# A routed expert stage in which one bias product per tile becomes two products in all, and two engines share the taking out of gathered tiles

## The reference, cut to what matters

```python
# x: 1024 tokens of 128, already normalised once and passed in as input_features
aff = x @ centroids.T                      # 8 affinities
assign = argmax(aff, axis=1)
xs, es = x[order], assign[order]           # order = argsort(assign)
alpha = sigmoid(aff of the chosen expert)
for e in range(8):
    h = layernorm(xs, ln_g[e], ln_b[e])
    h = relu(h @ w1[e].T + b1[e])          # 128 -> 512
    ye = xs + h @ w2[e].T + b2[e]          # 512 -> 128
    y += where(es == e, ye, 0)
out = alpha * y + (1 - alpha) * xs         # put back in the tokens' order
```

## Time and profile before

| | |
|---|---|
| runs | 1228.26, 1223.38, 1228.33 us; median 1228.26 |
| profiled execution | 1225.03 us, of which the span 1223.0 |
| mean granted TensorE clock | 0.918 |
| busy: PE, DVE, ACT, POOL | 1055.5, 809.7, 668.1, 389.4 us |
| the stage | from about 855 to 954 us |

### The profile page before, as it was taken

One profiled execution on the slowest core, in us unless ns is written; L12 is line 12 of the kernel. 1 busy time (PEld: TensorE's weight loads), 2 busy tenths in 40 slices (PEclk: granted clock), 3 DMA queues, 4 the chain that ended last, 5 costly groups with the idle time before them and its releaser, 6 DMA issues.

```text
span 1223.0 us, 18129 instructions
## 1 busy us (share of the span) xinstructions
PE 1055.5 (86%) x5958; PEld 737.6 (60%) x5958; DVE 809.7 (66%) x1975; ACT 668.1 (55%) x1640; POOL 389.4 (32%) x614
## 2 busy tenths in 40 slices
PE   3587899999958998789899999995799899997777
PEld 2345677777732333666677777774567566665665
DVE  5764588877757774558778786676734566666463
ACT  3253576676632667275677778773153366665021
POOL 5321112111111111143576566675200344444200
PEclk8687799999985989889899999997699999999879
DMA  6502000000023510210000000303200100000000
GB/s 216 107 21 91 1 1 14 1 1 1 1 68 101 190 29 2 87 52 1 1 1 1 1 1 1 139 1 147 101 1 1 70 1 1 1 2 1 1 1 18
DMA packets 26587, 45.08 MB, mean 37 GB/s; under 512 B 3544, under 2 KB 23808, under 8 KB 25216
## 3 DMA queue, kind: packets, MB, share of 16 engines
q1 hardware_dynamic: 23952, 41.58, 10.0%
q10 hardware_dynamic: 2544, 2.36, 0.6%
HBM read 36.95 MB, written 6.82 MB: 36 GB/s over the span
## 4 chain that ended last, share of the span: by engine, by line
PE 42%; ACT 9%; DVE 8%; issue 3%; POOL 2%; DMA 0%; SPq 0%; ACTq 0%; DVEq 0%; POOLq 0%
PE psum L1708 7%; ACT region_d L1774 4%; PE psum L2357 3%; PE psum L2325 2%; PE psum L2309 2%; PE psum L2292 2%; ACT region_c L1791 2%; PE psum L1745 2%; PE psum L1722 2%; PE psum L2287 2%; PE psum L987 1%; PE psum L1041 1%; PE psum L2368 1%; PE psum L2703 1%; PE psum L409 1%
## 5 line engine op out<-in xcount | busy, mean ns | idle before, releaser
L1708 PE MATMUL psum<-gated_parts 128*128 128x512 f32 x768 | 198.7, 411 | 15.1 <-DVE region_d L1878 11.0
L1708 PEld LDWEIGHTS psum<-gated_parts 128*128 128x128 f32 x768 | 141.2, 192 | 68.2 <-DVE region_d L1878 30.7
L1951 POOL TENSOR_TENSOR region_d<-region_d 128x256 f32<-128x256 f32 x128 | 101.0, 789 | 114.3 <-DVE region_d L1878 114.0
L1407 ACT ACTIVATE rounds_work<-psum,region_c 128x512 f32<-128x512 f32 x128 | 87.0, 689 | 59.4 <-PE psum L1322 59.4
L787 DVE TENSOR_REDUCE work<-psum 128x1 f32<-128x512 f32 x128 | 81.9, 685 | 27.8 <-PE psum L365 26.2
L1332 PE MATMUL psum<-parts,split 128*128 128x512 f32 x384 | 97.6, 404 | 0.0
L1774 ACT ACTIVATE region_d<-psum,gated_work 128x128 f32<-128x128 f32 x256 | 75.7, 450 | 36.8 <-issue 26.2
L1322 PE MATMUL psum<-parts,split 128*128 128x512 f32 x384 | 94.4, 396 | 0.0
L1477 DVE TENSOR_TENSOR parts<-rounds_work,parts 128x1024 fp32r<-128x1024 f32 x64 | 77.5, 1223 | 20.3 <-POOL parts L1563 17.4
L1563 POOL CAST parts<-rounds_work 128x1024 fp32r<-128x1024 f32 x32 | 33.4, 1045 | 179.8 <-ACT rounds_work L1407 179.8
L1878 DVE SCALAR_TENSOR_TENSOR region_d<-psum,gated_work,region_d 128x128 f32<-128x128 f32 x256 | 71.3, 344 | 29.0 <-ACT region_d L1774 24.7
(11 more groups left out here) (419 smaller groups left out, 2195.3 us busy)
## 6 DMA issues: line engine op xcount, KB each, us to landing
region_a<-in_l1v SPq DMA_DIRECT2D x1, 4096.0 KB, 14.3
region_b_last<-in_l1o SPq DMA_DIRECT2D x1, 4096.0 KB, 12.4
region_a<-in_l2f SPq DMA_DIRECT2D x1, 4096.0 KB, 13.6
region_b_last<-in_l3f_small SPq DMA_DIRECT2D x1, 4096.0 KB, 19.7
region_a<-in_l3f SPq DMA_DIRECT2D x1, 2080.0 KB, 7.5
region_c<-in_l0f SPq DMA_DIRECT2D x1, 2076.0 KB, 12.4
region_c<-in_l3x SPq DMA_DIRECT2D x1, 2048.0 KB, 7.8
ctx_parts<-front_work SPq DMA_DIRECT2D x6, 256.0 KB, 3.8
```

The source lines that it names most:

```text
L1407: act.activation(H[g % 2][:, f, :], bank[f], ACT.Gelu_apprx_tanh, bias=W("b1")[:, (g % E) * FT + f:(g % E) * FT + f + 1]).then_inc(h_ready ...
L1708: ins = pe.matmul(bank[2 * (n % 2) + c], src[a][:, t * P:(t + 1) * P], weights[b][:, piece(c)], start=m == 0, stop=m == len(PASSES) - 1)
L1951: pool.tensor_tensor(tile[:, 0:2, :], tile[:, 0:2, :], tile[:, 2:4, :], ALU.add).then_inc(k.pool_chain, 1)
```

## The change

It has four parts.

1. **Second bias.** The product L1030 of each tile, the row `one_row`, the row `b2_row` and its transfer on SP go. Instead PE transposes `chosen` with eight small bf16 products (new L989, each 8 x 128 out, into banks 6 and 7, with `ident16`, a new bf16 copy of the identity made by ACT), ACT copies the result to `chosenT` (8 experts x 1024 tokens, new L1085), and two fp32 products of the eight bias rows with `chosenT` (new L1014, 512 columns each) open the sums in banks 6 and 7 to which `back` adds. The slots product now also waits for `chosenT`'s copy, which frees banks 6 and 7.
2. **Taking out.** Tiles of banks 0 and 2 (0 to 3, 8 to 11) stay with ACT, tiles of banks 1 and 3 (4 to 7, 12 to 14) go to DVE. ACT loads all 15 expert registers ahead, as soon as `which` is there; DVE loads its seven ahead too.
3. **Banks.** `up` writes banks 4 and 5 in turn, `turn` writes bank 0. So `up(1)` needs only its own tile, and `turn(0)` needs tile 3 to be out of bank 0.
4. **Order on DVE.** The low parts of `xl` (L1133) come behind the choice. The matrices `rows_of(0)` and `rows_of(1)` are made ahead of the loop.

The core of the diff:

```diff
+    TAKEN_BY_ACT = [p for p in range(TILES) if p // (HALF // P) % 2 == 0]
+    TAKEN_BY_DVE = [p for p in range(TILES) if p // (HALF // P) % 2 == 1]
...
     def cols_of(g):
...
     def up_in(p):
-        return k.bank[0 if p % 2 else 4]
+        return k.bank[4 + p % 2]
+    def taken(p):
+        return act_took.at(TAKEN_BY_ACT.index(p) + 1) if p in TAKEN_BY_ACT else dve_took.at(TAKEN_BY_DVE.index(p) + 1)
...
     def y_in(p):
...
+        pe.wait_ge(*ident_ready.at(2))
+        for t in range(NT):
+            ins = pe.matmul(bank[6 + t // 4][0:E, (t % 4) * P:(t % 4 + 1) * P], chosen[:, t, :], ident16, start=True, stop=True)
+        ins.then_inc(chosenT_psum.semaphore, 1)
...
-                pe.wait_ge(*ident_ready.at(1))
+                pe.wait_ge(*chosenT_sb.at(1))
...
+        pe.wait_ge(*slot_sb.at(1))
+        for h in range(2):
+            pe.matmul(bank[6 + h], W("b2")[0:E, :], chosenT[0:E, h * HALF:(h + 1) * HALF], start=True, stop=False)
         def up(p):
...
-            pe.wait_ge(*taken.at(PER_BANK if p == 1 else p + 1))
+            pe.wait_ge(*taken(p))
...
+            else:
+                pe.wait_ge(*taken(PER_BANK - 1))
...
-                ins = pe.transpose(bank[5][:, f * P:(f + 1) * P], hsb[p % 2][:, f * P:(f + 1) * P], k.ident[:, :])
+                ins = pe.transpose(bank[0][:, f * P:(f + 1) * P], hsb[p % 2][:, f * P:(f + 1) * P], k.ident[:, :])
...
         def down(p):
...
-            if p == 0:
-                pe.wait_ge(*b2_loaded.at(16))
...
-                pe.wait_ge(*taken.at(PER_BANK * (p + 2)))
+                pe.wait_ge(*taken(PER_BANK * (p + 2) - 1))
...
-                pe.matmul(y_in(p), hT[p % 2][:, f * P:(f + 1) * P], w2[f][:, bass.ds(experts[p] * F, D)],
-                          start=f == 0, stop=False)
-            pe.matmul(y_in(p), one_row[0:1, :], b2_row[0:1, bass.ds(experts[p] * D, D)], start=False, stop=True)\
-                .then_inc(y_psum.semaphore, 1)
+                ins = pe.matmul(y_in(p), hT[p % 2][:, f * P:(f + 1) * P], w2[f][:, bass.ds(experts[p] * F, D)],
+                                start=f == 0, stop=f == FT - 1)
+            ins.then_inc(y_psum.semaphore, 1)
...
         def back(p):
...
-            if p == 0:
-                pe.wait_ge(*slot_sb.at(1))
...
-                                    start=p == 0 and i == 0, stop=p == TILES - 1 and i == 1)
+                                    start=False, stop=p == TILES - 1 and i == 1)
...
+        act.activation(ident16, k.ident[:, :], ACT.Copy).then_inc(ident_ready.semaphore, 1)
...
+        act.wait_ge(*chosenT_psum.at(1))
+        act.activation(chosenT[0:E, :].rearrange("p (a n) -> p a n", a=2), k.pair(6)[0:E, :, :], ACT.Copy)\
+            .then_inc(chosenT_sb.semaphore, 1)
...
-        experts = []
+        experts = [act.value_load(which[0:1, p:p + 1], min_val=0, max_val=E - 1) for p in range(TILES)]
...
         def take(p):
...
-            experts.append(act.value_load(which[0:1, p:p + 1], min_val=0, max_val=E - 1))
...
-                .then_inc(taken.semaphore, 1)
+                .then_inc(act_took.semaphore, 1)
...
         def hidden(p):
...
-                ins = act.activation(hT[p % 2][:, cols], bank[5][:, cols], ACT.Relu,
+                ins = act.activation(hT[p % 2][:, cols], bank[0][:, cols], ACT.Relu,
...
-        for p in range(2 * PER_BANK):
+        for p in TAKEN_BY_ACT[:PER_BANK]:
...
-            if p < GB - 2:
-                for q in range(PER_BANK * (p + 2), min(TILES, PER_BANK * (p + 3))):
+            if p == 0:
+                for q in TAKEN_BY_ACT[PER_BANK:]:
...
-        dve.wait_ge(*xl_high.at(1))
-        dve.tensor_tensor(xl_part[1], xl, xl_part[0].bitcast(F32), ALU.subtract).then_inc(xl_low.semaphore, 1)
...
+        dve.wait_ge(*xl_high.at(1))
+        dve.tensor_tensor(xl_part[1], xl, xl_part[0].bitcast(F32), ALU.subtract).then_inc(xl_low.semaphore, 1)
...
+        experts = {p: dve.value_load(which[0:1, p:p + 1], min_val=0, max_val=E - 1) for p in TAKEN_BY_DVE}
+        def take(p):
+            dve.wait_ge(*gathered.at(p // PER_BANK + 1))
+            dve.tensor_scalar(xs[:, p * P:(p + 1) * P], bank[p // PER_BANK][:, p % PER_BANK * P:(p % PER_BANK + 1) * P],
+                              W("g")[:, bass.ds(experts[p], 1)], W("b")[:, bass.ds(experts[p], 1)], ALU.mult, ALU.add)\
+                .then_inc(dve_took.semaphore, 1)
...
+        for p in range(2):
+            rows_of(p)
+        for p in TAKEN_BY_DVE[:PER_BANK]:
+            take(p)
...
         def take_up(p):
...
+            if p == 0:
+                for q in TAKEN_BY_DVE[PER_BANK:]:
+                    take(q)
...
-            if p < TILES:
+            if 2 <= p < TILES:
...
     def sync(sp):
-        first = sum(int(np.prod(shape)) for what, *shape in L2F_SMALL[:2])
-        sp.wait_ge(k.x_tiles, NT * (number - 1))
-        sp.dma_start(b2_row[0:1, :].rearrange("p (e d) -> p e d", e=E),
-                     k.dram["l2f_small"][0:E, first:first + D].unsqueeze(0)).then_inc(b2_loaded.semaphore, 16)
+        pass
...
```

More of the change, by code:

```diff
@@ L894, in sorted_experts @@
     slots_wide = k.mask_bc[:, :]
-    b2_row = k.carve(F32, E * D)
+    chosenT = k.carve(F32, T)
     tagged = k.carve(F32, NT, E)
@@ L902, in sorted_experts @@
     upto, ones = k.carve(BF16, P), k.carve(BF16, P)
-    one_row = k.carve(F32, P)
+    ident16 = k.carve(BF16, P)
     steps, firsts, slot_id = k.carve(F32, E), k.carve(F32, TILES), k.carve(F32, TILES)
@@ L924, in sorted_experts @@
     consts = k.count("packed_fill_done", 1)
-    ident_ready = k.count("packed_c_part", 1)
+    ident_ready = k.count("packed_c_part", 2)
+    chosenT_psum = k.count("packed_q_psum", 1)
+    chosenT_sb = k.count("packed_k_psum", 1)
     slot_ready = k.count("packed_c_rest", 1)
@@ L931, in sorted_experts @@
     gathered = k.count("experts_cwT_psum", GB)
-    taken = k.count("experts_cwT_sb", TILES)
+    TAKEN_BY_ACT = [p for p in range(TILES) if p // (HALF // P) % 2 == 0]
+    TAKEN_BY_DVE = [p for p in range(TILES) if p // (HALF // P) % 2 == 1]
+    act_took = k.count("experts_cwT_sb", len(TAKEN_BY_ACT))
+    dve_took = k.count("packed_av_out", len(TAKEN_BY_DVE))
     table_ready = k.count("packed_den_ready", 1)
@@ L945, in sorted_experts @@
     rows_psum = k.count("packed_wide_ready", 2)
-    b2_loaded = k.count("packed_nm_loaded0", 16)
     def cols_of(g):
@@ L1219, in gpsimd @@
         pool.memset(ones, 1.0)
-        pool.memset(one_row, 1.0)
         pool.memset(upto, 1.0)
```

## The result

The changed kernel takes 1217.65 us in the median of six runs (1216.34 to 1218.88), the kernel before 1227.7 (1223.38 to 1238.11). The ratio is 0.991, with a 95% interval of 0.988 to 0.994. The profiled execution has a span of 1216.0 against 1223.0 us.

The account below looks back on a forecast made before the run. PE's work was taken to bound the tile loop, with idle time and a low clock in the opening. Opening -2.05 and loop -5.75 us sum to -7.8, giving 1217.2 or 1220.5 by base; named 1218.5, range 1213.5 to 1224.

Parts of the forecast that it names:

- two bases: Starting times for the sum: the profiled execution's 1225.03 us, giving 1217.2, and the median 1228.26 us, giving 1220.5.
- One-row product: In the tile loop, removing the second-bias product saves its chain piece, 0.41 us per pass, 14 passes booked as 5.75 us.
- Upper end: those 0.5 us all go: In the tile loop, the most removal could save per pass: the time from L1028's streams ending to the way back.
- Rival A: In the tile loop, only 0.22 us per pass comes back, the rest being weight changes; 1220 to 1223.3 us, chance 0.14.
- Rival C: More than forecast: 0.5 us per pass and DVE's takes at 0.3; -9.8 us, 1213.6 to 1218.5 us, chance 0.10.
- Opening: From the gather's end to the second tile's down product: 2.05 us gained, tile 0's bias product included.
- ACT's loads: Fifteen hoisted register loads at 0.45 us each run from 880.2 to 887.1, covered by ACT's wait for gathering.
- the walk: Step-by-step timing of PE, ACT and DVE behind the gather, putting the second tile's down product at 899.05 against 901.10 us.
- Bias products: Two added fp32 products between gather and first up product, 1.72 us, cost nothing because PE is idle there.
- Choice of experts: Before the gather, moving the low parts behind the choice gains about 0.4, overruns by 0.3; net 0.1 us, booked nothing.
- Rival B: The opening gives nothing, through late DVE loads or takes or the 1.2 GHz level; -5.75 us, 1219.3 to 1222.5, chance 0.14.
- Rival D: Slower: opening pauses leave PE at 1.2 GHz in the loop, 6.6 us per pass; six passes give 1240 us, chance 0.03.

Follow-up runs that it names:

- runs 5 and 7: The changed kernel with all taking out on ACT, 1216.07 us; the changed kernel with DVE's register loads early, between the gather's matrices, 1216.49 us.
- run 6: The changed kernel with its two bias products moved from behind the gather to the first way back; 1221.51 us in one execution.
- run 4: The changed kernel with the low parts of x made ahead of the choice of experts again; 1221.93 us, ratio 0.994 to the kernel before.
- run 2: The kernel before without its one-row product, second bias left out, banks, order and taking out as before; 1220.6 us, ratio 0.995.
- run 9: The kernel before without its one-row product and with ACT's register loads ahead, banks and order as before; 1218.87 us in one execution.

## Why the prediction was right, and where its steps were off

The time lies 0.9 us from the forecast, and that is luck in part. The sum was -7.8 us; the stage fell by 11.3 and the median by 10. The forecast came near because 1218.5 was set 9.8 below the median of the three runs, between two bases. Of the 3.5 us by which the stage fell more than forecast, 2.7 are the loop (8.48 for 5.75), 1.3 the gather and 0.3 the choice of experts; the opening gave 0.8 less (1.29 for 2.05).

- **One-row product.** The mechanism, the place and the count held. The size didn't: 0.62 us per pass, above even the upper end of 0.5. The step that failed is "Upper end: those 0.5 us all go": it looked only up to where the way back starts and took its 1.13 us as its own. 0.20 of it belonged to the neighbour. 14 x 0.62 = 8.7 us, of which the table shows 8.48, where 5.75 was booked. Rival A was wrong in sign: the cost that comes from changing weights was the one-row product's, and went with it. **Rival C** had the direction right, with 0.5 per pass, and the time lies in its range too, so the time alone does not tell the forecast from it; the pass does.
- **Opening.** Booked 2.05 us, measured 1.29. The term mis-sized was DVE's loads: 4.62 us, 0.66 each in the mean, where ACT's rows had been taken to give 0.45 and 3.35 in all. Those rows were read short too: hoisted, ACT's loads came every 0.53 us. The matrices took 0.16 less than booked and the takes 0.33 less, so DVE's first copy, and with it the first turning, came 0.77 later behind the gather's end than in the walk. From there on the walk's times hold to 0.2 us, but one wait in it is another: it had the second turning wait for DVE's second copy, with ACT's hidden tile 0.15 ahead, and it waited for the hidden tile. What the prediction did not see is that the division, with DVE's loads where they stand, lost 1.5 us (runs 5 and 7).
- **Bias products** cost nothing in the change, shown by run 6, though only in part for the reason given. With its loads ahead ACT had its first tile out at 891.29, and PE could have started the first up product 1.1 us behind the gather's end; it started after 1.8, and the wait for DVE hid the rest. **ACT's loads** took 8.2 us instead of 6.9 and were covered all the same.
- **Choice of experts.** Booked 0, measured 0.3 (run 4).
- **Rival B** is half true: the low clock came into the opening in one of two profiles of the change and cost 1.3 us. **Rival D** did not come: at no time did it last into the loop.
- **The gather's** 1.3 us was not forecast. The clock rose 3.3 us after its start instead of 6.2. It can do so without the change: in run 2 it rose after 2.9, though in run 9 after 6.2. But all eleven profiles of the changed kernel and its variants have it between 2.8 and 3.5. Whether they have a part in it was not tested and stays open.

## What to carry to other kernels

When a small instruction is removed from a saturated engine, price it with what its neighbours pay for it: compare the neighbour's duration where it follows something else. Before dividing work over two engines, take the waits out of the one that has it; here ACT took a tile every 0.70 us with the register loads between and every 0.35 without, and with the loads ahead the division gained nothing. A second engine's share must be counted with its own queue ahead of it. And where a forecast comes out close, compare it stretch by stretch before trusting its terms.

## What was not expected of the hardware

A product of one row cost 0.62 us per pass where one of 128 rows, equal in columns, cost 0.24. Register loads with their following operations came every 0.53 us on ACT and every 0.61 on DVE, with 0.25 to 0.3 more behind the first of a row. The Trainium skill (DMA: Bandwidth & Descriptors, "Latency and other measured facts") gives some 600 ns as the floor of a tensor load; the instruction itself had a median of 275 ns on ACT and 299 on DVE here, so the trace does not agree.
